# GpSimd waits for the landing of all earlier scatters ahead of each unit's four, in the shared stage

## The reference

```python
x = x + xattn(layernorm(x), k, bias, ctx, ctx, 8)      # FFT convolution over 256 positions, per head
# ffn on t = layernorm(x):
scores = softmax(xt @ Wg.T)                            # 2048 tokens x 16 experts
topi = top_k(scores masked to the best 2 of 4 groups, 4)
h = silu(xt @ W1[e].T) * (xt @ W3[e].T)
y = sum over the 4 chosen e of  weight[e] * (h @ W2[e].T)
z = silu(xt @ Ws1.T) * (xt @ Ws3.T) @ Ws2.T            # the shared expert
x = x + y + z
```

## Time and profile before

| | us |
|---|---|
| median of three runs | 427.58 |
| the profiled execution | 428.87 |
| span of its trace | 427.1 |
| TensorE busy | 398.8 |
| VectorE busy | 233.5 |
| GpSimd busy | 198.6 |
| ScalarE busy | 176.9 |

### The profile page before, as it was taken

One profiled execution on the slowest core, in us unless ns is written; L12 is line 12 of the kernel. 1 busy time (PEld: TensorE's weight loads), 2 busy tenths in 40 slices (PEclk: granted clock), 3 DMA queues, 4 the chain that ended last, 5 costly groups with the idle time before them and its releaser, 6 DMA issues.

```text
span 427.1 us, 9265 instructions
## 1 busy us (share of the span) xinstructions
PE 398.8 (93%) x2157; PEld 296.2 (69%) x2158; DVE 233.5 (55%) x596; ACT 176.9 (41%) x543; POOL 198.6 (46%) x247
## 2 busy tenths in 40 slices
PE   6999999989999997399889999999999999999993
PEld 5888888878787454165476777777777777777772
DVE  3575788888786535127723444444444434443973
ACT  5348466546443530101103433344343334446662
POOL 3253323357786657376201433343343334346874
PEclk9999999999999999879999999999999999999999
DMA  7964655648879967144332344433343444478678
GB/s 241 341 219 151 223 174 184 225 160 294 268 247 356 298 235 269 71 158 159 110 99 69 119 132 130 126 125 128 122 130 118 134 120 128 135 227 259 225 251 305
DMA packets 45914, 79.69 MB, mean 187 GB/s; under 512 B 6144, under 2 KB 35168, under 8 KB 43840
## 3 DMA queue, kind: packets, MB, share of 16 engines
q1 hardware_dynamic: 39024, 59.57, 43.5%
q0 software_dynamic: 6864, 19.80, 11.9%
HBM read 54.95 MB, written 24.40 MB: 186 GB/s over the span
## 4 chain that ended last, share of the span: by engine, by line
PE 83%; DVE 4%; another core or an unknown queue 4%; issue 3%; DMA 2%; POOLq 1%; POOL 1%; ACT 1%; SPq 0%; DVEq 0%
PE heads L1221 21%; PE bank L1278 15%; PE heads L1129 12%; PE heads L1256 8%; PE heads L1131 6%; PE bank L1268 5%; PE bank L1244 4%; PE heads L1231 4%; PE bank L1143 4%; DVE kv L694 2%; PE bank L1154 2%; DMA toep<-toep_in 2%; PE bank L1170 1%; POOLq L671 1%
## 5 line engine op out<-in xcount | busy, mean ns | idle before, releaser
L663 POOL DMA_INDIRECT y_scratch<-toep,dest_i x64 | 61.5, 960 | 119.1 <-DVE dest_i L1002 114.6
L1221 PE MATMUL heads<-w,toep 128*128 x316 | 106.8, 460 | 1.6 <-ACT toep L473 1.1
L1129 PE MATMUL heads<-toep,kv 128*128 128x256 f32 x256 | 77.9, 386 | 4.9 <-DVE kv L694 2.2
L1278 PE MATMUL bank<-w,toep 88*128 x316 | 81.2, 379 | 0.0
L605 POOL DMA_INDIRECT rows_scratch<-rows,slot_i x64 | 64.1, 1001 | 28.8 <-issue 19.6
L1221 PEld LDWEIGHTS heads<-w,toep 128*128 128x128 f32 x316 | 53.6, 190 | 19.1 <-issue 2.3
L479 ACT ACTIVATE toep<-heads 128x176 f32<-128x176 f32 x79 | 25.0, 317 | 78.0 <-PE heads L1221 73.2
L1278 PEld LDWEIGHTS bank<-w,toep 88*128 88x128 f32 x316 | 53.8, 190 | 4.7
L1131 PEld LDWEIGHTS heads<-toep,kv 128*128 128x128 f32 x256 | 48.6, 190 | 6.6
L723 DVE TENSOR_TENSOR prod<-heads,ctx_rep 128x1024 f32<-128x1024 f32 x32 | 39.0, 1220 | 24.6 <-PE bank L1143 20.8
L1131 PE MATMUL heads<-toep,kv 128*128 128x128 f32 x256 | 49.2, 274 | 0.0
(11 more groups left out here) (180 smaller groups left out, 490.6 us busy)
## 6 DMA issues: line engine op xcount, KB each, us to landing
ctx_rep<-ctxr_in SPq DMA_DIRECT2D x16, 1024.0 KB
toep<-rows_scratch SPq DMA_DIRECT2D x65, 144.0 KB
w<-w_in SPq DMA_DIRECT2D x16, 352.0 KB
w<-w_in SPq DMA_DIRECT2D x16, 176.0 KB
rows_scratch<-pad_row SPq DMA_DIRECT2D x17, 144.0 KB
ctx_tr<-ctxt_in SPq DMA_DIRECT2D x16, 128.0 KB
toep<-toep_in SPq DMA_DIRECT2D x4, 512.0 KB, 8.5
ctx_n<-ctx_in SPq DMA_DIRECT2D x16, 128.0 KB, 2.0
```

What stands on the lines that cost most here:

```text
L663: pool.indirect_dma_start(y_d, bass.IndirectOffsetOnAxis(ap=dest.bitcast(U32), axis=0), y_sb[b], None).then_inc(y_sent[b], 16)
L1129: nc.tensor.matmul(y_ps[par][:, i, :], kv[:, q, 0, h * P:(h + 1) * P], toep[:, q * HH + h, :], start=True, stop=False)
L1221: last = nc.tensor.matmul(up_ps[p], x_tr[p][:, blk, :], w13[:, bass.ds(e, 1), blk, :].rearrange("p a n -> p (a n)"), start=blk == 0, stop= ...
L1278: last = nc.tensor.matmul(dn_ps[p], hid_tr[p][:, c, :], w2[:, bass.ds(e, 1), c, :].rearrange("p a n -> p (a n)"), start=c == 0, stop=c == 1)
```

## The change

One line is added, in GpSimd's program. Ahead of the four scatters of unit u, for u from 6 to 15, GpSimd waits until `scattered` has reached 64 u, that is until all 4 u scatters of the units in front have landed. The four scatters of one unit are still issued without a wait between them, and no instruction is moved, added or taken away otherwise.

```diff
@@ -648,6 +648,7 @@
             x_work(UNITS - 1)
             rstd2(UNITS - 1)
             for u in range(UNITS - ROUTE0 - TB, UNITS):
+                pool.wait_ge(scattered, 16 * TOPK * u)
                 scatter(u, range(TOPK))
```

## The result

The changed kernel takes 430.91 us (median of five, 430.73 to 432.45) against 427.58 (median of five, 426.37 to 427.83) for the kernel before: ratio 1.0103, 95% interval 1.0078 to 1.0127. By the medians it is 3.3 us slower, a quotient of 1.0078, which is the lower end of that interval; the interval reaches up to 5.4 us. Forecast were 424.9 us and a range of 420.5 to 430.

What follows compares the result with a forecast made beforehand. TensorE, 93% busy, plus its stalls was taken as the bound. `turn_x(0)` 5.0 us earlier less 2.3 for the clock gave -2.7, 426.2 for the profiled execution, 1.3 above the median: 424.9 us, range 420.5 to 430.

Steps and rivals of the forecast that it cites:

- the hold: Shared stage: news that the `up_shared(5)` matmuls were done at 166.45 reached ScalarE 12.4 us late, ending at 178.84.
- the change part: GpSimd's scatters: at most four in a row, then a 1.5 us gap, so no hold of more than a few us.
- the second rival: The hold has nothing to do with the scatters' run; TensorE hears at 178.8 as before: 427.6 us, chance 0.15.
- the first: Rival: the hold lasts as long as GpSimd has scatters, release at 187.5 against 178.8: +8.7, 436.3 us, chance 0.12.
- the chain of the scatters: GpSimd, units 6 to 15 with waits: units 9 to 15 every 6.26 us, last landing at 212.9, bounds 208 and 217.
- the 4.5 of the full queue: Landing time of a scatter behind a full DMA queue beside the weights: 4 to 5 us, taken as 4.5.
- such hitches: Two unexplained GpSimd delays after 181.68, 2.4 and 1.1 us: they add 3.5 unless the waits hide them; half taken.
- the clock's cost: TensorE at the routed stage's start: after standing 9 us its next matmuls run at half speed, 2.3 us back.
- The third rival: Landing slower than 2.2 us: 4.5 from unit 9 on gives near 439 us; mild form 428.5 to 432, chance 0.13.
- landing beside the weights: Scatters landing through a full queue while expert weights load: taken as 4.5 us.
- landing alone: Scatters landing with the queue otherwise empty: 2.2 us from start to landed, semaphore included.
- the rule on the queues: DMA engines take turns between queues packet by packet, so scatters shut nobody out and pacing would relieve nothing: 427.6 us.

Runs made afterwards that it cites:

- the two products: Kernel before, with two small GpSimd products, results unread, ahead of each unit's scatters from unit 6 on: 427.25 us, ratio 0.9996.

## Why the prediction was wrong

**What bounds the kernel** was read rightly: the hold, and its end in a release that has nothing to do with the multiplication. It goes when the scatters' run is cut up, as the change part assumed, and the second rival (the hold has nothing to do with the run) and the first (it lasts as long as GpSimd has scatters) fell: no wait marked "remote" is left after the change. `up_shared(6)` ended 1.5 us earlier than the 170.5 forecast, and TensorE's part ended at 203.4, forecast 204.9; both are the head start of 1.45 us of this execution.

**The step that failed is the chain of the scatters**, "last landing at 212.9, bounds 208 and 217". From the start of `up_shared(0)` that is 74.8 us; measured are 216.71 - 136.66 = 80.05, beyond the upper bound of 78.9. The 5.3 us are made up so:

- Units 6 to 8. Unit 9 was to start 29.2 us after `up_shared(0)` and started after 32.9: +3.7. Unit 6 itself started 0.7 late. From a unit's last scatter to the next unit's start the sum had 4.8 us behind unit 6 (4.5 to land and 0.3), 3.6 behind unit 7 (155.9 to 159.5) and 4.0 behind unit 8; measured are 5.83 (146.58 to 152.41), 6.58 (156.21 to 162.79) and 2.91 (166.62 to 169.53). Unit 7 is the largest single miss, 3.0 us: the 4.5 of the full queue was not even used for it.
- Units 9 to 15. The period was to be 6.26 us and was (210.46 - 169.53) / 6 = 6.82: +3.4. From a scatter's start to the landing that GpSimd sees is 2.46 us where I took 2.2, and three of the six periods were longer still: 7.05 and 6.83, and 7.46 ahead of unit 14, where GpSimd's unexplained idle time of 2.66 us turned up again. The waits hid most of it, since 1.77 would have passed there anyway: it cost 0.9, not 2.4. The long last scatter did not come back (0.96).
- The half of 3.5 us that I had kept for such hitches, 2.0 with the rounding, was thereby spent: -2.0. The last landing added 0.2.

From there on the steps were right: landing to gather 0.82 (0.8 forecast), gather to `turn_x(0)` 2.15 (2.1), the clock's cost 1.9 (2.3). With the right length of the chain the same sum gives 82.95 us to `turn_x(0)` instead of 77.7, and +0.4 + 1.9 = +2.3 for the change. The remaining 1.0 lies between the first send and the end, and there behind the last send: first to last send takes 192.5 us before and 192.6 after, the rest 4.6 and 5.5. Over the twelve traces the whole stretch is between 196.9 and 198.2 us, whatever the edit, so the 1.0 is no more than the spread of one execution. That this account adds up to the medians is in part luck, since the first stretch of the kernel before varies by 1.6 us too.

**The third rival** was the true case, in kind: slower landing, mild form, 428.5 to 432, at a chance of 0.13. The point from which it decides, a last landing at 215.6, was given correctly, and lay inside my own bounds. It was true in its outcome more than in its reason: it named units 9 on, which gave 3.4 of the 7.1 us too few, and units 6 to 8 gave the other 3.7. What was wrong was the weight: the two optimistic terms, landing beside the weights and landing alone, pointed the same way, and the 2.0 us kept for hitches did not cover them.

**What I had drawn from the rule on the queues** didn't hold either, though the rule is untouched. The Trainium skill, DMA: Bandwidth & Descriptors, section Queues, rings and completion order, lets each DMA engine take turns between queues. The trace of before agrees as far as that the scatters' 193 packets from 158 to 165 moved beside those of the weights; whether the turns are taken packet by packet no run here shows. The rival that I drew from it, that pacing would then relieve nothing, took for granted that only a full queue could make the hold. It is there at a DMA share of 0.31, and pacing relieved all of it.

## What to carry to other kernels

When a wait removes a stall, compute what is last next with the new waits in it, and let the errors of a chain of equal steps add up rather than cancel: ten steps that were on average half a microsecond too short made the whole error. Where one engine issues many indirect DMAs on end and others then hear late of finished work, try a gap first: here about 1.0 us after each four, or 1.86 after each eight, left delays of 2.4 us at most. Waiting for the landing left none, but its gap was 1.76 us at the least and up to 5.6 beside the weights, and that made the scatters the last thing in the stage. And an engine that is made to wait at the seam of two stages pays twice, once in the wait and once in its clock, unless something keeps it busy.

## What the runs showed of the hardware

Runs of indirect DMAs from GpSimd without a gap (a start every 1.26 us, 0.30 us between them) delayed the news of other engines' finished work: TensorE's by up to 12.4 us, VectorE's own by up to 1.8. It needs neither weight loads beside it nor a full queue, and it isn't there with a gap of 1.76 us or more after each four, whether a wait or other work on GpSimd makes the gap; with 1.0 us up to 1.7 us are left.

The length of the run is not the whole condition. All five runs of 16 (in four traces) made ScalarE hear 7.8 to 12.4 us late, and beside all six first runs of eight VectorE waited 2.3 to 2.8 us. But the kernel before has two more runs of eight, from 181.68 to 191.49 and from 194.15 to 205.52, and ScalarE hears in time beside both: the matmuls of `up_shared(7)` end at 190.69, and ScalarE starts at 190.72. Beside the run of twelve from 182.43 to 198.71 of the kernel with waits for units 6 to 11 and 96 transposes its waits are the usual 5.43 (with 16 transposes one is 0.6 us longer):

```profile
187.09 3.60 PE L1256 MATMUL heads<-xn_tr_all,ws 128*128 128x512 f32 x8
190.72 0.60 ACT L493 ACTIVATE prod<-heads 128x512 f32<-128x512 f32 x1 [10.81 <-issue]
...
190.60 0.60 ACT L493 ACTIVATE kv<-heads 128x512 f32<-128x512 f32 x1 [5.43 <-issue]
196.63 0.59 ACT L493 ACTIVATE prod<-heads 96x512 f32<-96x512 f32 x1 [5.43 <-issue]
```

The twelve from 176.67 to 192.06 of the kernel with waits ahead of units 9, 10 and 11 brought 3.9 us. What tells these runs apart is open. What in GpSimd or on the way of the semaphores is kept busy no trace here shows. Nor is it settled whether the length of the gap counts or that something other than a DMA stands in it: a gap of register work or of a different instruction was not tried.

TensorE's clock cost 1.9 us after an idle stretch of 14.5 us, but 4.2 us after one of only 8.1 us (all ten waits, and waits for units 6 to 11) and 1.8 after one of 7.5 (the two products). In the second case the tiles ran at the lower level until the third, in the other two only the first and the start of the second did. The length of the idle stretch alone doesn't tell the cost.
